# Row maxima from half-height products, two at a time, in an attention kernel with split operands

## The reference

```python
q = jnp.einsum('bnd,hed->bhne', xf, Wq)        # k and v alike, e = 64
s = jnp.einsum('bhqe,bhke->bhqk', q, k) / 8
mask = i[:, None] <= i[None, :] if lookahead else i[:, None] >= i[None, :]
s = jnp.where(mask, s, jnp.finfo(s.dtype).min)
p = jax.nn.softmax(s, axis=-1)
o = jnp.einsum('bhqk,bhke->bhqe', p, v)
```

## Time and profile before

| | before |
|---|---|
| time, median of 3 runs (lowest to highest) | 3432.36 us (3430.88 to 3432.69) |
| span of the profiled execution | 3431.4 us |
| PE busy | 3164.0 us, 92% |
| DVE busy | 2272.0 us, 66% (it has little to do in `project`) |
| ACT, POOL busy | 1744.9 us, 1542.0 us |
| granted TensorE clock, mean | 0.977 of full speed |

### The profile page before, as it was taken

The page is one execution under the profiler, slowest core; times in us unless marked ns, Lnnn a source line. Parts: engine busy times, 40 slices in busy tenths (PEclk is TensorE's granted clock), DMA queues, the critical chain, the costliest instruction groups (busy, mean ns, idle before and its releaser), DMA issues.

```text
span 3431.4 us, 53634 instructions
## 1 busy us (share of the span) xinstructions
PE 3164.0 (92%) x14472; PEld 2465.1 (72%) x14472; DVE 2272.0 (66%) x4412; ACT 1744.9 (51%) x3525; POOL 1542.0 (45%) x1626
## 2 busy tenths in 40 slices
PE   4999998999999589989999999999998999999998
PEld 3888887788888367767766677677776777767766
DVE  6212111310110599998998989998999899898996
ACT  2100101210100377777677777677777767776775
POOL 2000000100000466666666666676766666666663
PEclk9999999999999699999999999999999999999999
DMA  6234213422312222111121112111211112111210
GB/s 233 98 90 131 92 64 95 138 73 50 97 60 49 74 80 68 45 50 52 53 62 44 55 50 68 44 50 56 61 51 50 50 51 67 44 49 56 63 36 19
DMA packets 142566, 233.09 MB, mean 68 GB/s; under 512 B 76800, under 2 KB 76800, under 8 KB 142336
## 3 DMA queue, kind: packets, MB, share of 16 engines
q1 hardware_dynamic: 142336, 230.73, 22.3%
HBM read 163.58 MB, written 67.11 MB: 67 GB/s over the span
## 4 chain that ended last, share of the span: by engine, by line
PE 27%; DVE 13%; issue 13%; POOL 8%; ACT 4%; DMA 1%; POOLq 0%; DVEq 0%; ACTq 0%; SPq 0%
PE rows L1074 6%; POOL p_low L690 4%; PE max L1012 4%; DVE part_max L927 3%; PE scores L1042 3%; PE acc L1056 3%; PE acc L1060 3%; PE acc L1058 3%; DVE p_low L690 3%; PE scores L1037 3%; DVE o_full L981 2%; POOL k L715 2%; ACT p_high L863 2%; POOL v L718 2%; DVE inv L967 1%
## 5 line engine op out<-in xcount | busy, mean ns | idle before, releaser
L690 POOL TENSOR_TENSOR p_low<-probs,p_high 128x320 fp32r<-128x320 f32 (+3 forms) x1280 | 1072.6, 845 | 740.7 <-ACT p_high L863 678.9
L859 ACT ACTIVATE probs<-scores 128x512 f32<-128x512 f32 (+3 forms) x1280 | 686.6, 536 | 524.9 <-PE scores L1042 499.3
L927 DVE TENSOR_REDUCE part_max<-max 128x1 f32<-128x512 f32 (+3 forms) x1280 | 766.0, 599 | 83.2 <-PE max L1012 62.6
L863 ACT ACTIVATE p_high<-scores 128x512 fp32r<-128x512 f32 (+3 forms) x1280 | 685.6, 536 | 0.0
L1012 PE MATMUL max<-k,q 128*128 128x512 f32 (+3 forms) x1280 | 493.7, 387 | 164.7 <-DVE part_max L927 142.7
L690 DVE TENSOR_TENSOR p_low<-probs,p_high 128x192 fp32r<-128x192 f32 (+3 forms) x1280 | 634.2, 496 | 16.1 <-ACT p_high L863 14.2
L318 DVE COPY stage_d<-proj 128x512 f32<-128x512 f32 x96 | 66.0, 689 | 710.9 <-PE proj L264 461.1
L1042 PE MATMUL scores<-q,k 128*128 128x512 f32 (+3 forms) x1280 | 510.0, 398 | 0.0
L1056 PE MATMUL acc<-p_high,v 128*128 128x512 f32 (+3 forms) x1280 | 476.2, 372 | 9.4 <-issue 6.4
L1037 PE MATMUL scores<-q,k 128*128 128x512 f32 (+3 forms) x1280 | 475.2, 371 | 4.4 <-ACT p_high L863 4.3
L1060 PE MATMUL acc<-p_low,v 128*128 128x512 f32 (+3 forms) x1280 | 473.3, 370 | 0.0
(11 more groups left out here) (94 smaller groups left out, 4981.7 us busy)
## 6 DMA issues: line engine op xcount, KB each, us to landing
raw<-qk_s SPq DMA_DIRECT2D x256, 256.0 KB, 4.2
xs<-xT SPq DMA_DIRECT2D x64, 512.0 KB, 4.8
w_raw<-wqk SPq DMA_DIRECT2D x32, 512.0 KB, 3.6
qk_s<-stage_a SPq DMA_DIRECT2D x64, 256.0 KB, 2.4
qk_s<-stage_d SPq DMA_DIRECT2D x64, 256.0 KB, 2.4
raw<-v_s SPq DMA_DIRECT2D x64, 256.0 KB, 2.8
res<-x_res SPq DMA_DIRECT2D x32, 512.0 KB, 4.1
out<-res SPq DMA_DIRECT2D x32, 512.0 KB, 2.6
```

The source lines that it names most:

```text
L690: eng.tensor_tensor(p_low[:, n % 4, part], probs[:, n % 4, part], p_high[:, n % 4, part].bitcast(F32), ALU.subtract).then_inc(done, 1)
L859: nc.scalar.activation(probs[:, n % 4, 0:cols], scores[n % 2][:, 0:cols], ACT.Exp, scale=SCALE).then_inc(exp_done, 1)
L863: nc.scalar.activation(p_high[:, n % 4, 0:cols], scores[n % 2][:, 0:cols], ACT.Exp, scale=SCALE).then_inc(high_act, 1)
L927: nc.vector.tensor_reduce(part_max[:, s % 2, at, m:m + 1], max_bank[n % 2][:, 0:cols], AX.X, ALU.max).then_inc(max_read, 1)
```

## The change

The products for the maxima contract over 64 rows instead of 128. Units 2m and 2m + 1 are issued together in the turn of the even unit: the even one takes partitions 0 to 63 of `q1` and `k1`, the odd one partitions 64 to 127 of `q1` and `k2`. Both are q high by k high, so k low no longer enters the maxima. To have k high in the lower half of `k2`, the two halves of `q2` and `k2` change places: the shift's row and the ones are now in partition 0, q low and k high in 64 to 127. One wait stands ahead of the pair: all units before the even one have been read. The order on DVE, ACT, POOL and SP stays row for row what it was.

```diff
@@ split_low
             if u < 2:
-                ins = eng.tensor_tensor(q2[0:E, p, cols], raw[0:E, slot, src],
-                                        q1[0:E, p, cols].bitcast(F32), ALU.subtract)
+                ins = eng.tensor_tensor(q2[E:P, p, cols], raw[E:P, slot, src],
+                                        q1[E:P, p, cols].bitcast(F32), ALU.subtract)
@@ gpsimd
-                nc.gpsimd.memset(q2[E:P, p, :].bitcast(F32), 0.0).then_inc(cleared, 1)
-                nc.gpsimd.memset(k2[E:P, p, :].bitcast(F32), 0.0).then_inc(cleared, 1)
+                nc.gpsimd.memset(q2[0:E, p, :].bitcast(F32), 0.0).then_inc(cleared, 1)
+                nc.gpsimd.memset(k2[0:E, p, :].bitcast(F32), 0.0).then_inc(cleared, 1)
...
-                nc.gpsimd.memset(k2[E:E + 1, p, :].bitcast(F32), 1.0).then_inc(cleared, 1)
+                nc.gpsimd.memset(k2[0:1, p, :].bitcast(F32), 1.0).then_inc(cleared, 1)
@@ scalar
-                        nc.scalar.activation(k2[0:E, p, cols], raw[0:E, slot, src], ACT.Copy)
+                        nc.scalar.activation(k2[E:P, p, cols], raw[E:P, slot, src], ACT.Copy)
...
-                    nc.scalar.activation(q2[E:E + 1, p, qb * NQ:(qb + 1) * NQ], side[E:E + 1, :],
+                    nc.scalar.activation(q2[0:1, p, qb * NQ:(qb + 1) * NQ], side[0:1, :],
                                          ACT.Copy).then_inc(shift_ready, 1)
@@ tensor
-                if step == "max":
-                    _, _, _, qc, key, cols, _ = max_unit(kind, n)
+                if step == "max" and n % 2 == 0:
                     if n == 0:
 
                         pe.wait_ge(low_split, count(i, p, SPLITS, 8))
 
-                    reached(pe, max_read, count(i, p, M_UNITS, n - 1))
-                    to = max_bank[n % 2]
-                    nc.tensor.matmul(to[:, 0:cols], q1[:, p, qc * P:(qc + 1) * P],
-                                     k1[:, p, key:key + cols], start=True, stop=True).then_inc(max_scored, 1)
+                    reached(pe, max_read, count(i, p, M_UNITS, n))
+                    for m, part, keys in ((n, slice(0, E), k1), (n + 1, slice(E, P), k2)):
+                        _, _, _, qc, key, cols, _ = max_unit(kind, m)
+                        nc.tensor.matmul(max_bank[m % 2][:, 0:cols], q1[part, p, qc * P:(qc + 1) * P],
+                                         keys[part, p, key:key + cols], start=True, stop=True).then_inc(max_scored, 1)
```

## The result

| | before | after |
|---|---|---|
| time, median of 4 runs each (lowest to highest) | 3431.62 us (3426.64 to 3432.69) | 3607.26 us (3603.24 to 3609.32) |
| span of the profiled execution | 3431.4 us | 3604.0 us |

A forecast was written before the change was run, and what follows sets the result against it. PE and DVE, both above 90% busy in attention, were taken to bound the kernel by holding each other up. 3431.4 + 61 (wait) + 4 (prologue) + 70 (mode changes) = 3566 us, 3567 for the median; range 3465 to 3655.

The forecast's parts named there:

- The wait: Before each pair, PE waits until both banks are read: net 1.9 us a head, 61 us, plus 4 in the prologue.
- The prologue: No `p_low` there covers DVE's standstill, so each of the 11 later pairs adds about 0.4 us: +4 us.
- the lead at turns 9 and 31: The pair needs a later reading there, so PE falls behind: net +0.61 and +0.36 us a head.
- the round trips: DVE stands still between pairs where it leads, in turns 1, 21 and 25: 0.3 us each, +0.9 a head.
- The change of mode: PE goes from full array to halves and back, 40 times a head: 20 x 0.11 = 2.2 us a head, 70 us.
- my other factor, half of the pairs: The price of going to halves and back counts only where PE is late, turns 9 to 19 and 31 to 37.
- The saving: On PE a pair costs only its wider unit: 3.4 us a head, 107 us, counting only where PE is late.
- rival 2: Second rival, chance 0.15: halves do not overlap and each move between full array and halves costs 0.16 us: 3634 us.
- Free parts: Copies, subtractions and memsets on 64 other partitions, same columns, unchanged order on DVE, ACT, POOL and SP: counted as nothing.
- The first rival: Going between full array and halves costs nothing, both halves run freely, only the waits remain: 3497 us, chance 0.25.
- The third: Rival: PE is late nearly everywhere, the pair's wait is harmless, two thirds of 107 us is saved: 3361 us, chance 0.12.
- the fourth: Rival: over the whole kernel gain and loss cancel, within 0.2%: 3432 us, chance 0.03.

The follow-up runs named there:

- same_half: The changed kernel with both products of a pair in the same half, partitions 0 to 63: 3670.64 us, ratio 1.0700.
- pair_full: The kernel before, with both units of a pair issued together after one wait for both banks, each at full height (128 rows): 3550.11 us, ratio 1.0341.
- half_single: The changed kernel with pairs taken apart: every unit over 64 rows, in its own turn with its own wait: 3714.46 us, ratio 1.0825.
- strict_wait: The kernel before, one full-height unit a turn, but each waits until the unit just before it has been read: 3600.12 us, ratio 1.0497.
- moved_only: The kernel before with only the partitions moved, products for the maxima still over 128 rows, one a turn: 3451.53 us, ratio 1.0056.
- moved_src64: The kernel before with the partitions moved, but the copy of the shift's row still reads partition 64 and writes partition 0: 3432.86 us, ratio 1.0006.
- before_src0: The kernel before with one edit: the shift's row is read from partition 0, still written to partition 64: 3430.32 us, ratio 1.0000.

## Why the prediction was right, and where not

The direction and the mechanism held, and 3607 lies in the range. It is 40 us above the 3567 that I named. By the steps:

**The wait.** The pair does start 0.05 us after the later reading in turns 1, 5, 9, 15, 21, 25, 29 and 31, nearly every head, and in turn 9 the round trip is 0.60 us. I had put it at 1.9 us a head after taking off some 1.0 of savings, 2.9 gross. At full height it measures 3.3 (8410 matmuls in the 2000 us, so 73.3 us a head for 70.0). The prologue, from its first unit to the first scores, grew from 25.1 to 30.8 us, 5.7 for my 4. Of my gross 98 us, some 64 are the lead at turns 9 and 31, where the odd unit's early place measures 60, and some 33 the round trips with the prologue, where the single wait measures 58: that term was short. The two splits are alike, not the same, since the single wait can also hold back PE in turns 9 and 31. The places came out right in part. In the changed kernel, mode changes included, turns 7 to 10 lengthened by 1.6 us where I had worked out 1.05. Turns 31 to 38 added 1.4 for my 0.36, turns 20 to 30 added 1.2 for two round trips of 0.3, and turns 11 to 19, which were to give back 0.44, added 1.0. (Turn 31's lateness is 0.93 by its rows, not 0.94; nothing hangs on it.)

**The change of mode.** This is the term that was mis-sized. I took 0.11 us a change, "the nearest thing that a row shows, a weight load that isn't hidden". It is two such steps, 0.20 us. My upper end of 0.16, the tail of a matmul's record, was no upper end. On the path it made 121 us (`same_half` over `pair_full`, which also holds the moved partitions), where I had 70 and at most 102. That is 3.8 us of the 20 x 0.40 = 8.0 that PE pays a head, so my other factor, half of the pairs, held.

The Trainium skill's "TensorEngine Tiling (Array Packing)", Key Properties, has TensorE drained at a change of tiling mode, which spoke for this side. The runs agree on the side; they show the price and not what happens inside.

**The saving.** The halves overlap as hoped, 3 ns apart. It brought 63 us of the 107 that it takes off PE. I had credited it with 0.44 + 0.58 = 1.0 us a head, 33 us (1.1 and 35 in rival 2).

The Trainium skill's "TensorE: Matmul & The Clock Gate", Part 3, has matmuls in different row groups start some 4 ns apart, and the trace agrees.

**Free parts.** The moved partitions cost nothing as such, but the faster copy of the shift's row did by itself, through a collision of DVE and POOL: 20 us, on a kernel whose timing is that of before. In the changed kernel the copy is as fast, but this collision is not there: its `p_low` lasts 0.36 us in turn 26 and 0.45 in turn 27, for 0.82 and 0.92 with the partitions alone moved. Whether the copy has some other share was not tried.

The steps from before to after are: order 60, the single wait 58, mode changes 121, overlap -63, together 176 us. They run from one kernel to the next, so that they add up to the whole is no proof of them; what each stands for is shown by its own run. Against my terms the waits were 21 us above, the changes of mode 51 above, and the saving took off 30 more. So two misses cancel in part, which is luck; with the saving as I had it, the sum would be near 3637, still in the range.

The first rival, free changes of mode (3497 us), fell with `half_single`. The second had the price too low as well (0.16) and was wrong about the overlap, yet its 3634 is nearer to 3607 than my 3567: the time alone doesn't decide between us, the 3 ns and `same_half` do. The third, that the wait is harmless, fell with `pair_full`, and the fourth with the result.

The granted clock over the 2000 us of attention went from 0.99 to 0.98. After 1300 us it stood at half speed, its 1.2 GHz level, for 67 us before the change and for 102 us after it. Of the 28 heads from the third to the thirtieth, those with less than 1 us at half speed take 69.4 us before (12 of them) and 74.2 us after (5), against 69.9 and 74.9 for all 28. So by an estimate from these means the clock makes 0.2 of the 5.0 us a head, some 7 us in all. What brings the drops was not taken apart.

## What to carry to other kernels

- Count what a packed pair pays at its borders before counting what it saves: here 0.40 us against at most 0.23. A pair is too short a stay in the half mode. By these prices two full-width pairs in a row would about break even (0.46 against 0.40, an estimate that no run tried), and here there are banks for one.
- When two buffers are refilled by one step, the step waits for both, and double buffering is gone. `strict_wait` shows what lead is worth without any pair: 5% for one unit.
- Before calling an edit free because its durations hardly change, look at the starts as well, and for two engines that block each other. The copy's record was 0.02 us shorter, but what followed it came 0.30 us sooner, and that decided which of two engines started first.

## What the runs showed of the hardware

- Full array to half-height products and back: 0.09 to 0.11 us on each of the next two matmuls, at each change, with 512, 384 and 256 columns alike (`half_single`).
- Two half-height products in different halves start 3 ns apart and take the time of one; in the same half they take that of two (0.335 us apart).
- A subtraction of two SBUF tensors on DVE (192 columns) takes 0.33 to 0.36 us when POOL is idle at its start. When POOL's own subtraction (320 columns) is running then, it nearly always ends 0.21 to 0.34 us after that one's end, so its length depends on how much of POOL's is left: 0.33 to 1.07 us in the kernel before, 0.84 and 0.98 in the collisions of `moved_only`.
- ScalarE's copy of one row of 512 from PSUM to SBUF takes 0.570 us if both are at partition 0, and 0.587 to 0.591 if one or both are at 64. From the start of the operation ahead of it to that of the operation behind it, it is 0.95 us in the first case and 1.25 to 1.26 in the second (`moved_only` and after; before, `moved_src64` and `before_src0`).
